# Feed-forward weight rounding moved to other steps of the cross-attention loop, and the splits ahead of that loop shared by two engines

## The reference

```python
x = x + latent_attention(layernorm(x), ...)            # 16 heads of 128 + 64 rotary, causal
x = x + cross_attention(layernorm(x), ctx_2048, mask)  # 16 heads of 16; clip(scores, -50, 50), softmax over 1500
x = x + ffn(layernorm(x), w_gating, w_linear)

# cross attention
k, v = ctx @ Wk.T + bk, ctx @ Wv.T + bv
probs = softmax(where(mask, clip(q @ k.T / 4, -50, 50), -50))
delta = clip(residual_scale, 0, 0.3) * ((probs @ v) @ Wo.T + bo)
delta = layernorm(delta) * gamma + beta
# ffn: both operands of each product are rounded to E4M3 first
out = qdot(gelu(qdot(x, w_gating[0])) * qdot(x, w_gating[1]), w_linear)
```

## Time and profile before

| | |
|---|---|
| median of the runs | 1648.18 us |
| profiled execution | 1649.31 us, of which the span of the trace is 1647.4 us |
| TensorE matmul busy | 1521.0 us (92%) |
| VectorE busy | 1374.1 us (83%) |
| ScalarE busy | 1107.0 us (67%) |
| GpSimd busy | 637.8 us (39%) |

### The profile page before, as it was taken

One profiled execution on the slowest core, in us unless ns is written; L12 is line 12 of the kernel. 1 busy time (PEld: TensorE's weight loads), 2 busy tenths in 40 slices (PEclk: granted clock), 3 DMA queues, 4 the chain that ended last, 5 costly groups with the idle time before them and its releaser, 6 DMA issues. The chain is left out here.

```text
span 1647.4 us, 43930 instructions
## 1 busy us (share of the span) xinstructions
PE 1521.0 (92%) x18002; PEld 1293.7 (79%) x18002; DVE 1374.1 (83%) x2423; ACT 1107.0 (67%) x2099; POOL 637.8 (39%) x655
## 2 busy tenths in 40 slices
PE   5999999998869999999999999999999999999446
PEld 5888888887548888888888888888888888888224
DVE  3788888898538898998988989989889898898587
ACT  2666666665447777777777777777777777776475
POOL 0466656565143343333333433333334333332014
PEclk9999999999979999999999999999999999999677
DMA  7000000000041112111121122111121111110001
GB/s 228 7 1 2 1 1 1 2 1 1 1 120 52 46 45 58 58 40 58 51 58 54 44 58 58 41 57 52 58 58 40 52 51 50 42 52 2 1 12 34
DMA packets 44504, 67.90 MB, mean 41 GB/s; under 512 B 9557, under 2 KB 42770, under 8 KB 44178
## 3 DMA queue, kind: packets, MB, share of 16 engines
q1 hardware_dynamic: 44306, 65.11, 13.8%
HBM read 63.26 MB, written 1.84 MB: 40 GB/s over the span
## 5 line engine op out<-in xcount | busy, mean ns | idle before, releaser
L1243 POOL TENSOR_TENSOR xa_CW<-xa_CTX,xa_CH 128x500 fp32r<-128x500 f32 x187 | 242.5, 1297 | 504.7 <-DVE xl_ACC L1482 420.1
L1438 ACT ACTIVATE xl_PB<-banks,xl_BIB,xl_SCB 125x896 f32<-125x896 f32 x384 | 401.0, 1095 | 38.1 <-PE banks L1290 38.1
L1482 DVE TENSOR_TENSOR xl_ACC<-xl_ACC,xl_PB 125x896 f32<-125x896 f32 x320 | 374.4, 1170 | 11.0
L1473 DVE TENSOR_SCALAR xl_PB<-xl_PB 125x896 f32<-125x896 f32 x384 | 315.6, 825 | 47.6 <-ACT xl_PB L1438 46.3
L1256 PE MATMUL banks<-xa_WVhigh,xa_CH 128*125 128x256 f32 x768 | 234.7, 306 | 0.0
L1420 ACT ACTIVATE xl_V<-banks 125x512 f32<-125x512 f32 x192 | 115.0, 599 | 177.1 <-PE banks L1256 177.0
L1256 PE MATMUL banks<-xa_WVhigh,xa_CW 128*125 128x256 f32 x768 | 216.2, 282 | 0.0
L1256 PE MATMUL banks<-xa_WVlow,xa_CH 128*125 128x256 f32 x768 | 216.0, 281 | 0.0
L1489 DVE SCALAR_TENSOR_TENSOR xl_KXlow<-banks,xa_bk,xl_KXhigh 128x500 fp32r<-128x500 f32 x192 | 137.0, 713 | 70.0 <-ACT xl_KXhigh L1411 70.0
L1306 PE MATMUL banks<-xl_PB,xl_V 125*32 125x112 f32 x6144 | 167.5, 261 | 1.9 <-DVE xl_PB L1473 1.9
L1256 PEld LDWEIGHTS banks<-xa_WVhigh,xa_CH 128*125 128x125 f32 x768 | 142.5, 186 | 27.2 <-issue 16.3
(11 more groups left out here) (238 smaller groups left out, 3696.1 us busy)
## 6 DMA issues: line engine op xcount, KB each, us to landing
xa_CTX<-in_ctxT SPq DMA_DIRECT2D x96, 500.0 KB, 3.6
fw_QUT<-in_W_quT SPq DMA_DIRECT2D x1, 2048.0 KB, 12.9
fw_WO<-in_W_o SPq DMA_DIRECT2D x1, 2048.0 KB, 18.6
xl_RAW<-in_w_gating SPq DMA_DIRECT2D x8, 256.0 KB, 4.0
X<-in_x SPq DMA_DIRECT2D x1, 1792.0 KB, 9.4
out<-ff_R SPq DMA_DIRECT2D x16, 112.0 KB, 1.9
xl_RAW<-in_w_linear SPq DMA_DIRECT2D x4, 256.0 KB, 4.0
QThigh<-in_ku SPq DMA_DIRECT2D x1, 520.0 KB, 12.9
```

The source lines that it names most:

```text
L1243: nc.gpsimd.tensor_tensor(context_piece(CW, i), context_piece(CTX, i), context_piece(CH, i), ALU.subtract).then_inc(ctx_low, 1)
L1438: nc.scalar.activation(PB[t % PR][:, :, :], banks[0:TK, 2 * i:2 * i + KT, 0:QW], ACT.Exp, scale=SCB[j][:, t:t + 1], bias=BIB[j][:, t:t + 1 ...
L1473: nc.vector.tensor_scalar(pt, pt, E_HI, E_LO, ALU.min, ALU.max).then_inc(clipped, 1)
L1482: nc.vector.tensor_tensor(ACC[j][:, :, :], prev[:, :, :], PB[t % PR][:, :, :], ALU.add).then_inc(summed, 1)
```

## The change

Inside the loop, ScalarE's `half_weights` moves from the end of step 8 to the end of step 7. VectorE's `weight_step` 0 (`TF`) moves into step 8, between `xl_CR` and the second clip; step 1 (`CF` clamped) to the end of step 8, ahead of `keys_low`; step 2 (the rest) into step 10, between the first add and the second clip, where step 1 stood; step 3 moves from step 3 to step 4 of the next pair, both times ahead of the second clip.

Between the loops, VectorE takes the low part of `WV` and the low parts of context pieces 1 and 3 from GpSimd, which keeps `WK` and pieces 0, 2 and 4; ScalarE makes four high context parts ahead of the queries and one behind them, in place of two and three.

```diff
@@ cross_queries, VectorE
+                dve.wait_ge(high_ready, 2)
+                nc.vector.tensor_tensor(WV[1][:, :, :], WV0[:, :, :], WV[0][:, :, :], ALU.subtract).then_inc(wv_low, 1)
                 for m in range(KT):
+                    i = 1 + 2 * m
+                    dve.wait_ge(ctx_high, i + 1)
+                    nc.vector.tensor_tensor(context_piece(CW, i), context_piece(CTX, i), context_piece(CH, i), ALU.subtract).then_inc(odd_low, 1)
                     dve.wait_ge(q_high, m + 1)
...
@@ cross_queries, GpSimd
-                for i, (parts, whole) in enumerate(((WK, WK0), (WV, WV0))):
-                    pool.wait_ge(high_ready, i + 1)
-                    nc.gpsimd.tensor_tensor(parts[1][:, :, :], whole[:, :, :], parts[0][:, :, :], ALU.subtract).then_inc(low_ready, 1)
-                    pool.wait_ge(low_ready, i + 1)
-                for i in range(MADE):
+                pool.wait_ge(high_ready, 1)
+                nc.gpsimd.tensor_tensor(WK[1][:, :, :], WK0[:, :, :], WK[0][:, :, :], ALU.subtract).then_inc(low_ready, 1)
+                pool.wait_ge(low_ready, 1)
+                for k, i in enumerate(range(0, MADE, 2)):
                     pool.wait_ge(ctx_high, i + 1)
                     nc.gpsimd.tensor_tensor(context_piece(CW, i), context_piece(CTX, i), context_piece(CH, i), ALU.subtract).then_inc(ctx_low, 1)
-                    pool.wait_ge(ctx_low, i + 1)
+                    pool.wait_ge(ctx_low, k + 1)
@@ cross_queries, ScalarE
-                for i in range(2):
+                for i in range(4):
                     context_high(i)
...
-                for i in range(2, MADE):
+                for i in range(4, MADE):
                     context_high(i)
@@ cross_loop, ScalarE
-                        if s == 8 and piece_in(g) is not None:
+                        if s == 7 and piece_in(g) is not None:
                             half_weights(piece_in(g))
@@ cross_loop, VectorE, ahead of clip(n, 1, ...)
-                        if s == 10 and piece_in(g) is not None:
-                            weight_step(piece_in(g), 1)
-                        if s == 3 and piece_in(g - 1) is not None:
+                        if s in (8, 10) and piece_in(g) is not None:
+                            weight_step(piece_in(g), s - 8)
+                        if s == 4 and piece_in(g - 1) is not None:
                             weight_step(piece_in(g - 1), 3)
@@ cross_loop, VectorE, ahead of keys_low
-                        if s in (9, 10) and piece_in(g) is not None:
-                            weight_step(piece_in(g), 2 * (s - 9))
+                        if s == 8 and piece_in(g) is not None:
+                            weight_step(piece_in(g), 1)
```

More of the change, by code:

```diff
@@ L992, in cross_queries @@
         mask_step, rs_step, high_ready, low_ready, ctx_low = sem("mask_step"), sem("rs_step"), sem("high_ready"), sem("low_ready"), sem("ctx_low")
+        wv_low, odd_low = sem("wv_low"), sem("odd_low")
         with nc.Block() as block:
```

## The result

The kernel after takes **1655.22 us**, the median of 5 runs (1654.84 to 1656.71). The kernel before, on the same chip, took 1650.12 (5 runs, 1646.86 to 1654.18; the three behind the 1648.18 above are among them). The ratio is 1.0034, with a 95% interval of 1.0017 to 1.0050: 0.34% slower, inside the 0.5% that the prediction called hard to tell from no change. 1653.8 was predicted. The profiled execution of after took 1655.08 us, its span is 1653.3.

A forecast was written before the change was run, and what follows sets the result against it. TensorE bounds the loop, waiting 12 times for GpSimd's `CW` (5.5 us). 12 x (0.55 + 0.13) = +8.2 us, less 2.6 between the loops, gives +5.6: 1653.8 us; 8-in-10 range 1644 to 1658.

The forecast's parts named there:

- Step 8: In weight pairs, two added VectorE operations make `CW` late; step 9 grows by 0.55 us (0 to 0.7).
- Step 10: In weight pairs, one VectorE operation exchanged; step 11 grows by 0.59 us in place of 0.46, net +0.13.
- Edits at nothing: In the loop, moving the sum to step 4 and `HF` ahead of step 8's exponentials costs 0.
- Between the loops: Stage ahead of the loop: the mask follows one GpSimd `CW`, not three; gain 2.6 us (1.3 to 4.3).
- half of the gain: At the loop's start, if TensorE's clock rises no sooner than now, only 1.3 us of the stage's gain stays.
- Rival 1: In the loop, waits for `CW` go away; loop gains 5.5 us, stage 2.6: 1640.1 us; chance 0.07.
- Rival 2: In step 8, no exclusion by the clamp and `TF`; keys only 0.08 us late: 1649.1 us; chance 0.12.
- Rival 3: In the loop, the wait only changes place, 12 x (0.55 - 0.46) = 1.1 us: 1646.7 us; chance 0.05.
- Rival 4: `HF` ahead of step 8's exponentials adds 0.28 us to clip, adds and both late `CW`: 1657.1 us; chance 0.12.

The follow-up runs named there:

- e3_half_back: The kernel after with ScalarE's `half_weights` back at the end of step 8; 1656.08 us in one run.
- e5_tf_only: The kernel after with only `TF` moved into step 8, clamp and rest in step 10 as in before; 1658.77 us in one run, weight pair 66.27 us.
- e4_no_beta: The kernel after without GpSimd's addition of `BET` in step 8; 1649.30 us in one run, weight pairs 65.89 us.

## Why the prediction was right

The mechanism and the places held, and the sum came out near: 8.2 less 2.6 predicted, 7.3 less 2.0 measured. That 5.6 and 5.3 are so close is in part luck, as the cost was set 0.9 too high and the gain 0.6 too high. On the medians it is 5.1. The 1653.8 was added to the 1648.18 of three runs; five runs gave 1650.12.

- **Step 8** (+0.55 predicted): step 9 grew by 0.56. `CW` and the keys came at the moment worked out. Without `BET`'s addition it is +0.01, without the clamp +0.33.
- **Step 10** (step 11 +0.59 predicted): it grew by 0.54, where it had grown by 0.47 in most pairs of before. So the net is 0.07, not 0.13. This is the term that was mis-sized: 12 x 0.06 = 0.7 us of the 8.2.
- **Edits at nothing**: `HF` and the sum in step 4 cost nothing (`e3_half_back`; no step but 9 and 11 changed).
- **Between the loops** (-2.6, bounds 1.3 to 4.3): 3.0 sooner at the first key, 2.0 at the first scores. GpSimd's side gave more than two `CW`, as its last wait for ScalarE ended 0.5 us earlier against the stage's start (11.8 for 12.3 us), which the prediction had at the same time; the clock took 1.0 back. The prediction had named that loss (half of the gain) and then chose the value without it. Over all profiles, the old stage took 27.6, 27.8 and 26.5 us to the first scores, the new one without extra matmuls 24.5 to 25.6 (six of them, mean 25.1): 2.2 us in the mean.
- **The rivals.** Rival 1, that the waits go away in these even steps, fell: 24 waits. It was right in one respect: there are even steps where they go away (0, 2, 4 and 6), but in 8 and 10 GpSimd has an operation of the normalization beside the second clip (rows above), and they have the least room, 0.25 us in step 8. Rival 2 (no exclusion by `TF` and the clamp) fell by the rows: GpSimd's addition ends 0.59 behind `TF`, and `CW` takes 1.51 behind the clamp and 1.29 without it (`e5_tf_only`); for the clip, `e4_no_beta` shows the exclusion directly. Rival 3 would have left 0.09 a pair; it was 0.62. Rival 4 fell by `e3_half_back`.

The span grew by 5.9 us: the 5.3 of the two terms, 0.7 ahead of the change and 0.1 less behind it.

## What to carry to other kernels

Work moved to another step of a pipelined loop cost nothing here where its delay was smaller than the room behind the result that the busiest engine waits for; so first make a table of that room step by step, and put the work where it is largest. VectorE's same four operations cost 1.1 us a pair in steps 8, 8, 10 and 4, 0.47 in 9, 10, 10 and 3, and nothing in 2, 4, 6 and 0. Where VectorE and GpSimd both work in SBUF, count for each meeting the whole of the other's operation; and where TensorE idles ahead of a loop, see at which clock it comes back before a gain in the stage ahead is counted in full.

## What the runs showed of the hardware

- The operations of VectorE and GpSimd named here exclude each other rather than share. A clip of 0.62 us takes 1.17 beside a GpSimd addition and 0.62 when that is taken away; `CW` takes 1.28 alone and 1.49 to 1.51 behind a clamp that began 0.04 to 0.06 before it. The Trainium skill says it so, in "Trainium Architecture — The Big Picture", section "What this means for kernel authors": the contention of that pair is an exclusive lock and not a split of bandwidth; the trace agrees, with the numbers above. `keys_low`, which reads a bank of PSUM, took no more than 0.74 us beside a GpSimd operation in any kernel.
- Between the loops VectorE's subtraction of 128x500 takes 0.67 us alone and 1.41 beside GpSimd's, 1.17 beside the low part of `WK`. The engine that began second ended 0.53 to 0.55 us behind the other's end. So the two took turns here too: what the stage gained came from where its last operations stand, not from two engines working at once.
- TensorE came back at the lower clock behind pauses of 3.7 us and more, and at the higher behind 0.6 and 0.4. The granted clock rose 3.0 to 5.9 us behind the first key in the kernels that came back at the lower one; the way from the first key to the first scores was 7.0 to 8.4 us in them, so that alone moves the first scores by over 1 us from one execution to the next.
